# Cross attention and a routed FFN on one core: two 64-row down products put side by side in the array, with a second copy of their weights

## The reference

```python
logits = x @ gate_weight.T
probs = softmax(logits)
top_val, top_idx = lax.top_k(probs, 8)          # then renormalised, secondary experts rerouted
xs = x[tok]                                     # tokens in order of their expert
gu = lax.ragged_dot(xs, swapaxes(gate_up_proj, 1, 2), group_sizes)   # 512 -> 2 * 192
gate, up = split(gu, 2, axis=-1)
hact = silu(gate) * up                                               # 192 features
y = lax.ragged_dot(hact, swapaxes(down_proj, 1, 2), group_sizes)     # 192 -> 512
out = zeros_like(x).at[tok].add(y * w[:, None])
```

## Time and profile before

| | |
|---|---|
| median of 3 runs | 769.99 us (768.62 to 772.36) |
| the profiled execution, its own time | 767.57 us |
| its span in the profile | 765.8 us |
| PE busy | 661.4 us, 86% of the span |
| PEld, DVE, ACT, POOL busy | 72%, 71%, 60%, 71% |
| DMA engines, mean over the span | 248 GB/s |

### The profile page before, as it was taken

One profiled execution on the slowest core, in us unless ns is written; L12 is line 12 of the kernel. 1 busy time (PEld: TensorE's weight loads), 2 busy tenths in 40 slices (PEclk: granted clock), 3 DMA queues, 4 the chain that ended last, 5 costly groups with the idle time before them and its releaser, 6 DMA issues. The chain is left out here.

```text
span 765.8 us, 15219 instructions
## 1 busy us (share of the span) xinstructions
PE 661.4 (86%) x4278; PEld 554.9 (72%) x4278; DVE 542.6 (71%) x1213; ACT 456.7 (60%) x891; POOL 541.9 (71%) x463
## 2 busy tenths in 40 slices
PE   4999999831079999999999999999999999999920
PEld 2565555531069988888889999999999999889720
DVE  5598998865047666666677888888887887788611
ACT  3454454312036667667677877778777877768611
POOL 7007777777675877787788888878877888888521
PEclk9999999955579999999999999999999999999975
DMA  8999998615377999999999999999999999999576
GB/s 300 359 326 319 326 349 287 238 44 173 88 208 174 250 230 228 238 227 243 233 246 269 302 289 296 282 273 278 275 274 270 276 274 270 266 273 272 101 143 152
DMA packets 107589, 189.97 MB, mean 248 GB/s; under 512 B 33537, under 2 KB 35457, under 8 KB 106097
## 3 DMA queue, kind: packets, MB, share of 16 engines
q1 hardware_dynamic: 74274, 125.61, 52.0%
q0 software_dynamic: 33232, 63.39, 38.4%
HBM read 143.43 MB, written 56.24 MB: 261 GB/s over the span
## 5 line engine op out<-in xcount | busy, mean ns | idle before, releaser
L1256 PE MATMUL bank<-xh,w1h 128*128 128x256 f32 (+7 forms) x768 | 225.9, 294 | 3.6 <-issue 2.1
L1258 PE MATMUL bank<-xh,w1l 128*128 128x256 f32 (+7 forms) x768 | 220.0, 286 | 0.0
L1257 PE MATMUL bank<-xl,w1h 128*128 128x256 f32 (+7 forms) x768 | 219.9, 286 | 0.0
L617 POOL DMA_INDIRECT xg<-normed_tokens,list x145 | 170.9, 1179 | 59.6 <-issue 55.4
L601 POOL DMA_INDIRECT list_table<-token,slot x112 | 111.6, 996 | 74.4 <-issue 73.7
L626 POOL DMA_INDIRECT out_rows<-ys,list x73 | 123.1, 1686 | 39.7 <-issue 20.1
L1256 PEld LDWEIGHTS bank<-xh,w1h 128*128 128x128 f32 x768 | 147.0, 191 | 4.3 <-issue 4.2
L1257 PEld LDWEIGHTS bank<-xl,w1h 128*128 128x128 f32 x768 | 147.3, 192 | 0.1
L1258 PEld LDWEIGHTS bank<-xh,w1l 128*128 128x128 f32 x768 | 146.9, 191 | 0.0
L626 POOL DMA_INDIRECT second_sum<-ys,list x70 | 117.6, 1680 | 30.3 <-issue 18.6
L922 DVE TENSOR_TENSOR w1l<-raw,w1h 128x1536 fp32r<-128x1536 f32 x65 | 114.3, 1759 | 17.7 <-ACT w1h L1073 16.2
(11 more groups left out here) (205 smaller groups left out, 1115.0 us busy)
## 6 DMA issues: line engine op xcount, KB each, us to landing
raw<-in_w SPq DMA_DIRECT2D x195, 256.0 KB, 5.4
raw<-in_w2a SPq DMA_DIRECT2D x65, 256.0 KB
ctxT_s<-in_ctxT SPq DMA_DIRECT2D x16, 768.0 KB, 7.1
ctx_s<-in_ctx SPq DMA_DIRECT2D x16, 768.0 KB, 8.6
raw<-in_w2b SPq DMA_DIRECT2D x65, 128.0 KB
list_table<-blank SPq DMA_DIRECT2D x30, 256.0 KB, 7.4
x_in<-in_x SPq DMA_DIRECT2D x16, 224.0 KB, 5.3
out_rows<-x SPq DMA_DIRECT2D x16, 224.0 KB, 8.3
```

The costliest lines, as they stand in the source:

```text
L617: pool.indirect_dma_start(xg[u.on(XGS)][0:u.m, t, :], None, normed, bass.IndirectOffsetOnAxis(ap=lists[u.on(LISTS)][0:u.m, t, 0:1], axis=0 ...
L1256: pe.matmul(bank[m][:, 0:W], wh, mh, start=(c == 0), stop=False)
L1257: pe.matmul(bank[m][:, 0:W], wh, ml, start=False, stop=False)
L1258: mm = pe.matmul(bank[m][:, 0:W], wl, mh, start=False, stop=(c == DK - 1))
```

## The change

In `down`, a unit with more than one tile (all 63 static ones) begins with the fifth products of its first two tiles, each over 64 rows: tile 0 uses rows 0 to 63 of `hl[:, 1]` and of `w2h[:, 1]`, tile 1 uses rows 64 to 127 of `hl[:, 1]` and of a new tensor `w2r`. The two write different banks. Then each of these tiles has four products over 128 rows; a third tile keeps its five. The low part of `hl` by the low part of the rest weights, a product of two small parts that L1274 computed along, is left out for the two tiles. The waits for the free banks of both tiles stand ahead of the pair. In `w2_high`, ACT makes one copy more, the high rest weights into rows 64 to 127 of `w2r`.

```diff
@@ -263,6 +263,7 @@
         early.close()
         w2h.append(sb("w2h1", [P, 2, D], F32R))
         w2l.append(sb("w2l1", [P, D], F32R))
+        w2r = two("w2r", [P, D], F32R)
         w1h.append(sb("w1h1", [P, DK, 2 * F], F32R))
@@ -1078,6 +1079,7 @@
                 b = u.on(2)
                 raw = raw2[u.on(RAW2)]
                 a.copy(w2h[b][:, 0, :], raw[:, 0, :])
+                a.copy(w2r[b][FR:P, :], raw[0:FR, 1, :])
                 a.copy(w2h[b][0:FR, 1, :], raw[0:FR, 1, :]).then_inc(w2h_s, 1)
@@ -1262,16 +1264,25 @@
                 b = u.on(2)
                 pe.wait_ge(hl_s, u.n + 1)
                 pe.wait_ge(w2l_s, u.n + 1)
+                beside = range(2 if u.nt > 1 else 0)
+                for t in beside:
+                    wait(pe, ys_s, freed_before(u, t, 3))
+                for t in beside:
+                    half = slice(t * FR, (t + 1) * FR)
+                    rest = w2r[b][half, :] if t else w2h[b][half, 1, :]
+                    pe.matmul(y_bank(u, t)[0:u.m, :], hl[b][half, 1, t * u.m:(t + 1) * u.m], rest, start=True, stop=False)
                 for t in range(u.nt):
-                    wait(pe, ys_s, freed_before(u, t, 3))
+                    alone = t not in beside
+                    if alone:
+                        wait(pe, ys_s, freed_before(u, t, 3))
                     s = slice(t * u.m, (t + 1) * u.m)
                     o = y_bank(u, t)[0:u.m, :]
-                    pe.matmul(o, hh[b][:, 0, s], w2h[b][:, 0, :], start=True, stop=False)
+                    pe.matmul(o, hh[b][:, 0, s], w2h[b][:, 0, :], start=alone, stop=False)
                     pe.matmul(o, hh[b][:, 0, s], w2l[b][:], start=False, stop=False)
                     pe.matmul(o, hl[b][:, 0, s], w2h[b][:, 0, :], start=False, stop=False)
-
-                    pe.matmul(o, hh[b][:, 1, s], w2h[b][:, 1, :], start=False, stop=False)
-                    pe.matmul(o, hl[b][:, 1, s], w2h[b][:, 1, :], start=False, stop=True).then_inc(y_ps, 1)
+                    if alone:
+                        pe.matmul(o, hl[b][:, 1, s], w2h[b][:, 1, :], start=False, stop=False)
+                    pe.matmul(o, hh[b][:, 1, s], w2h[b][:, 1, :], start=False, stop=True).then_inc(y_ps, 1)
```

## The result

The changed kernel takes 775.88 us (median of 9 runs, 774.49 to 780.51), the kernel before 768.75 us in the same runs (9, 765.74 to 772.36). The ratio is 1.010 with a 95% interval of 1.0077 to 1.0123, so the change costs 6 to 9 us. The forecast was slower, 782 us, with a range of 772 to 793. The direction and the price of the two passages came as forecast; the sum was about twice too large, since the two halves start together and the units of three tiles mostly pay nothing.

The account below looks back on a forecast made before the run. TensorE was taken to bound the unit loop. Per unit, 0.184 + 0.18 + 0.09 - 0.234 = 0.22 us lost, times 63 is 13.9 us; added to 767.57 or the median 769.99 this gives 781.5 or 783.9, said as 782, range 772 to 793.

Parts of the forecast that it names:

- the two passages: PE's array going from 128 rows to 64 and back, each unit: weight loads wait, losing 0.184 us in, 0.18 out.
- the sum: Per unit on PE: 0.184 + 0.18 + 0.09 - 0.234 = 0.22 us lost, times 63 is 13.9 us.
- What lies between the two products of the pair: Gap between the two 64-row products on PE: taken as 0.09 us, one open load, between nothing and 0.234.
- the estimate by it, 8.4 us: Total loss if the pair's matmuls start about 4 ns apart, as the Trainium skill says, instead of 13.9 us.
- the lower bound that the text gave: With nothing between the pair's two products, a unit loses 0.13 us, 8.2 us in all.
- TensorE sets the time there: In the unit loop, 212 to 725 us, PE is busy 503.84 of 513 us and bounds the time.
- 63 times: What PE gains or loses in a unit moves the end equally in all 63 units, unless a hidden stall emerges.
- The copy and the bank waits counted as nothing: ACT's 0.51 us copy per unit falls in idle time and waits ahead of the pair are free: 0 us.
- Faster (no emptying): Rival: passages to 64 rows don't empty the array, loads stay pulled forward; 753 to 759 us, chance 0.09.
- the half of it: Rival: only one of the two passages empties the array, no real change; 764 to 770 us, chance 0.08.
- the halves don't stream together: Rival: the pair's two products stream one after the other; 22.9 us more, 790.5 us, chance 0.12.
- ACT late for `hl`: Rival: in the last 24 units each new copy delays PE, adding 12 us to the main sum; 793 us, chance 0.04.

Follow-up runs that it names:

- the two kernels with the turn moved: Third tile of three-tile units turned one block later, on the kernel before (763.33 us) and on the changed kernel (771.37 us).
- the two together: Changed kernel with its two early fifth products over all 128 rows, new order and extra ACT copy kept: 771.81 us, ratio 1.0041 against the kernel before.

## Why the prediction was right, and where its sum was off

**The two passages: right.** In and out, the loads start only 0.07 to 0.08 us before the recorded end of the matmul ahead and then stand in the open, as the earlier trace rows of the first part had shown for 2 and 16 rows. The prediction had the load of the pair 0.204 us behind the last gate and up product (measured 0.20) and 0.414 us from the pair's streaming to the next. The pair's recorded 0.48 us hold its open load of 0.09, for a product with a hidden load is recorded with 0.39; so the pair streams from about 545.15. The first 128-row product streams 0.234 us ahead of the second, from 545.80 - 0.234 = 545.57, and between the two are 0.42 us. The run with the halves apart gives 0.18 us for a passage, the same as the sum's terms.

**What lies between the two products of the pair: mis-sized.** The prediction took 0.09 us, "one open load", from two loads of 128 rows that followed each other. The pair's loads start together and its matmuls 0.01 us apart or less. The nearest row was of loads into the same rows of the array and said nothing of two halves. The Trainium skill's distance of some 4 ns between matmuls of different row groups ("TensorE: Matmul & The Clock Gate", Part 3) agrees with these rows, and the estimate by it, 8.4 us, came nearer. With nothing between, the unit loses 0.13 us, the lower bound that the text gave; measured are 0.13 by the timeline above and 7.64 - 7.47 = 0.17 in units of two tiles of 128.

**"TensorE sets the time there", and what PE loses moves the end "63 times": the step that failed.** It holds in the 46 units of two tiles and not in most of the 17 of three. There PE's down products run beside a longer chain that goes through DVE and ends in `xl`; the period is 10.61 us before and after, with one product less and with 0.36 us more. From the rest silu of the fourth unit to that of the sixteenth, twelve periods, it is 122.81 us in both kernels (255.43 to 378.24 before, 259.38 to 382.19 after). From that of the seventeenth unit to that of the last static one, 46 periods, it is 334.55 us before (387.31 to 721.86) and 340.17 after (391.41 to 731.58), 5.6 us more. In the two kernels with the turn moved it is 333.47 and 340.17, 6.7 us more, and there ACT's list of waits has none for weights behind 290 us. The prediction had read the waits as small (2.8 us for `xl`) and missed that the same wait came back in each of these units, each time with a part covered by a matmul's end. So the sum is 46 units and not 63, at 0.13 to 0.17 us, 6 to 8 us, and the measured change is 6 to 9. The total alone would not tell this from 63 units at 0.13 us, 8.2 in all; the periods do.

**The copy and the bank waits counted as nothing: right each by itself**, by the runs with the copy alone (1.0002) and the order alone (1.0008). ACT's idle time in front of the rest silu took the copy up. For the two together, 1 to 5 us, the cause stays open.

**The rivals.** Faster (no emptying) and the half of it are excluded by the timelines of both passages. That the halves don't stream together is excluded by the run with both in one half, 0.23 us a unit longer. ACT late for `hl` is excluded by PE's waits for it, which fell from 1.6 to 0.7 us.

## What to carry to other kernels

A pair of halves in the array saves one product, but in the middle of 128-row work it has to pay for two passages, here 0.18 us each against 0.234 us saved. By these numbers, as an estimate that no run here shows, two pairs between the same two passages would save 0.1 us. What a product is worth has to be read by stage: in a stage where a chain on another engine closes in each unit, PE's work beside it is free up to the slack, here some 0.4 us a unit, however busy PE looks. Before an edit of the busiest engine, leaving the work out costs one run and tells what the edit can bring at most, here 0 to 4 us.

## What the runs showed that was not expected

Two loads into different halves of the rows start at the same time (545.06 and 545.06), while loads into the same rows, where they stand in the open, follow one another by some 0.10 us (545.47 to 545.57 for all rows, and the two of the run with both in one half). A wait that the list gives as 0.25 us was a gap of 0.39 us in the stream of starts. And 0.24 us less PE work in each unit brought almost nothing late in the loop, while the waits for weights grew by 15 us and those for output rows by 12.
